# Gated layer with overlapping tiles and ternary matrices on three engines, statistics-operation norms, and first keys split over VectorE and ScalarE with joined stores

## The reference

```python
def _layernorm(x, axis=-1, eps=1e-05):
    m = jnp.mean(x, axis=axis, keepdims=True)
    v = jnp.var(x, axis=axis, keepdims=True)
    return (x - m) / jnp.sqrt(v + eps)
...
        q = _fq_sym(q, axis=-1)
        k = _fq_sym(k, axis=-1)
        v = _fq_sym(v, axis=2)
...
            w_dq = jnp.clip(jnp.round(w / gamma_w), -1.0, 1.0) * gamma_w
...
        gate = jax.nn.silu(bit_linear(x, gate_w, gate_b))
        val = bit_linear(x, val_w, val_b)
        return bit_linear(gate * val, out_w, out_b)
```

## Time and profile before

| | us |
|---|---|
| median of 3 runs | 6873.82 |
| lowest, highest | 6869.46, 6882.35 |
| profiled execution, its own time | 6872.02 |
| its span in the trace | 6870.2 |
| busy PE, DVE, ACT, POOL | 5802.4, 5704.3, 4387.7, 3741.3 |

### The profile page before, as it was taken

The page is one execution under the profiler, slowest core; times in us unless marked ns, Lnnn a source line. Parts: engine busy times, 40 slices in busy tenths (PEclk is TensorE's granted clock), DMA queues, the critical chain, the costliest instruction groups (busy, mean ns, idle before and its releaser), DMA issues. The chain is left out here.

```text
span 6870.2 us, 178673 instructions
## 1 busy us (share of the span) xinstructions
PE 5802.4 (84%) x63503; PEld 2380.6 (35%) x63510; DVE 5704.3 (83%) x8942; ACT 4387.7 (64%) x4251; POOL 3741.3 (54%) x3973
## 2 busy tenths in 40 slices
PE   2771699999999999999999999999949487999523
PEld 2331133333333333333333333333334353544311
DVE  5886699999999999999999999999943556777655
ACT  0330089988989889989889989989912013666301
POOL 2331078888888888878888888888810001000000
PEclk7995599999999999999999999999969697999756
DMA  1442211011011011011011011011020078877500
GB/s 57 112 108 94 46 22 18 9 26 19 9 26 19 9 26 18 10 26 18 10 26 18 11 25 19 11 25 19 10 48 0 19 303 181 116 112 114 85 28 9
DMA packets 182852, 319.86 MB, mean 47 GB/s; under 512 B 97220, under 2 KB 143813, under 8 KB 176803
## 3 DMA queue, kind: packets, MB, share of 16 engines
q1 hardware_dynamic: 181944, 307.93, 21.0%
HBM read 196.59 MB, written 113.33 MB: 45 GB/s over the span
## 5 line engine op out<-in xcount | busy, mean ns | idle before, releaser
L1024 DVE TENSOR_REDUCE a_mx<-PS 128x1 f32<-128x512 f32 x6620 | 4073.2, 688 | 230.1 <-PE PS L908 226.5
L995 ACT ACTIVATE a_e<-PS,a_sk 126x1024 f32<-126x1024 f32 x3264 | 3634.0, 1114 | 458.2 <-PE PS L893 109.6
L771 POOL TENSOR_SCALAR a_p<-a_e 126x1024 f16<-126x1024 f32 x3264 | 3418.1, 1047 | 641.0 <-ACT a_e L995 588.5
L908 PE MATMUL PS<-a_K,a_Q 48*128 48x512 bf16 (+1 forms) x6884 | 2109.8, 383 | 49.9 <-DMA a_K<-d_inv 49.9
L893 PE MATMUL PS<-a_Q,a_K 54*126 54x512 bf16 x6528 | 2113.3, 404 | 26.6 <-issue 17.4
L935 PE MATMUL PS<-a_e,a_sel 126*32 126x256 f32 x26112 | 1994.7, 382 | 0.0
L893 PEld LDWEIGHTS PS<-a_Q,a_K 54*126 54x126 bf16 x6528 | 615.4, 131 | 1377.3 <-issue 1319.6
L931 PE MATMUL PS<-a_p,a_V 128*32 128x256 f16 x13056 | 960.1, 284 | 14.1 <-ACT a_og L976 10.0
L931 PEld LDWEIGHTS PS<-a_p,a_V 128*32 128x32 f16 x13056 | 336.8, 93 | 1251.6 <-POOL a_p L771 1059.0
L935 PEld LDWEIGHTS PS<-a_e,a_sel 126*32 126x32 f32 x26112 | 756.1, 110 | 8.9 <-issue 2.4
L1891 DVE TENSOR_REDUCE b_mx<-PS 128x1 f32<-128x512 f32 x803 | 504.8, 685 | 188.4 <-PE PS L1775 188.4
(11 more groups left out here) (300 smaller groups left out, 3363.9 us busy)
## 6 DMA issues: line engine op xcount, KB each, us to landing
b_K<-d_k SPq DMA_DIRECT2D x210, 200.1 KB, 6.1
a_K<-d_k SPq DMA_DIRECT2D x102, 400.2 KB
d_v<-v1v SPq DMA_DIRECT2D x9, 3328.0 KB, 10.3
b_V<-d_v SPq DMA_DIRECT2D x36, 832.0 KB, 12.1
d_k<-k_T SPq DMA_DIRECT2D x400, 63.0 KB, 1.7
d_k<-k1p SPq DMA_DIRECT2D x54, 400.2 KB, 7.7
a_V<-d_v SPq DMA_DIRECT2D x68, 204.0 KB, 2.8
d_v<-vq SPq DMA_DIRECT2D x17, 803.2 KB
```

The source lines that it names most:

```text
L771: g.tensor_scalar(p[0:rows, kk % RE, :], e[0:rows, kk % RE, :], 1.0, SHIFT, ALU.mult, ALU.add).then_inc(rounded, 1)
L908: last = pe.matmul(self.PS[:, M_BANK + j % sh.SLOTS, c0:c0 + wd], Qb[M_ROWS, ii % 4, t * P:(t + 1) * P], Kb[M_ROWS, (ii // NC) % 2, k0:k0 ...
L995: a.activation(e[0:r, kk % RE, :], self.PS[0:r, e_bank(i, s):e_bank(i, s) + 2, :], ACT.Exp, scale=skb[0:r, hb, s:s + 1]).then_inc(exp_done, 1)
L1024: v.tensor_reduce(mx[:, col:col + 1], bank, AX.X, ALU.max).then_inc(max_done, 1)
```

## The change

Norms: 16 statistics operations and 16 aggregations give mean and variance, and 16 instructions apply both. First keys: the key scales are found straight from PSUM; a third, bf16 product of three bias rows adds the bias on TensorE; both bf16 casts and the copies of the values (plain and absolute) go to ScalarE; VectorE keeps a running largest value; the turn of a group comes one group later; the four parts share two banks, and a group is stored by three DMAs. First values: the largest values come from the running ones, are turned by TensorE and spread by a product with ones; scaling, rounding and storing go by halves and heads. First attention: the first keys come in five pieces, and GpSimd clears the 34 semaphores of the stages so far ahead of its buffers. Gated layer: the three matrices have buffers of their own, ScalarE scales them, GpSimd clips them, all beside the norm; in the main loop ScalarE takes the value half from PSUM, GpSimd adds its bias, and product and final step of a tile come one tile later.

```diff
+    def norm_sums(self, v, nm):
+        for t in range(self.sh.NT):
+            self.mark(v.bn_stats(nm["parts"][:, t, :], self.x[:, t, :]), self.dv)
+        v.wait_ge(self.dv, self.count[id(self.dv)])
+        for t in range(self.sh.NT):
+            self.mark(v.bn_aggr(nm["mean_var"][:, t, :], nm["parts"][:, t, :]), self.dv)
+        v.wait_ge(self.dv, self.count[id(self.dv)])
+        v.tensor_scalar(nm["st"][:, 2, :], nm["mean_var"][:, :, 1], EPS, None, ALU.add).then_inc(self.var_ready, 1)
...
+            self.mark(v.tensor_scalar(xn[:, t, :], self.x[:, t, :], nm["mean_var"][:, t, 0:1], st[:, 0, t:t + 1],
+                                      ALU.subtract, ALU.mult), self.dv)
...
+                    for c in range(2):
+                        sp.dma_start(self.d_k0[:, 8 * c:8 * c + 8, :, g * GW:g * GW + n].rearrange("i h d n -> (h d) i n"),
+                                     kT[:, g % 2, :, c, 0:n]).then_inc(stored[g % 2], 16)
...
+                    for y in range(2):
+                        for j, n in tiles(g):
+                            kv = self.PS[0:n, 2 * (g % 2) + y, j * D:(j + 1) * D]
+                            for c in range(2):
+                                pe.matmul(kv, cT[:, g % RC, c, j * KT:j * KT + n], W[:, c, y * D:(y + 1) * D],
+                                          start=(c == 0), stop=False)
+                            last = pe.matmul(kv, pick[0:96, 0:n], bp[0:96, y * D:(y + 1) * D], start=False, stop=True)
...
+                        self.link(v, v.tensor_reduce(sc, by_head(ps), AX.X, ALU.max, apply_absolute_value=True), self.dv)
...
+                    v.wait_ge(cast, 2 * g + 1)
+                    for s, n in spans(g):
+                        self.link(v, v.tensor_tensor(tmp2[0:n, b, s, :], kf[0:n, b, s, :], parts[0:n, b, HI, s, :], ALU.subtract), self.dv)
+                    v.sem_inc(to_cast, 1)
...
+                def largest(g):
+                    v.wait_ge(v_taken, g + 1)
+                    for s, n in spans(g):
+                        top = self.v_top[0:n, s, :]
+                        self.link(v, v.tensor_tensor(top, v_abs[0:n, g % 2, s, :], top, ALU.max), self.dv)
...
+                    scales(g)
+                    if g >= 1:
+                        rest(g - 1)
+                    whole(g)
+                    if g >= 1:
+                        last(g - 1)
+                    scaled(g)
+                    largest(g)
+                rest(NG - 1)
+                last(NG - 1)
...
+                    a.wait_ge(to_cast, 2 * g + 1)
+                    a.activation(parts[0:KT, g % 2, HI, :, :], kf[0:KT, g % 2, :, :], ACT.Copy).then_inc(cast, 1)
...
+                        ins = a.activation(parts[0:n, g % 2, MID, s, :], tmp2[0:n, g % 2, s, :], ACT.Copy)
...
+                        a.activation(self.v_raw[0:n, g * GT + s.start:g * GT + s.stop, :], ps, ACT.Copy)
+                        ins = a.activation(v_abs[0:n, g % 2, s, :], ps, ACT.Abs)
+                    ins.then_inc(v_taken, 1)
...
+                for g in range(NG):
+                    if g >= 3:
+                        evacuate(g - 3)
+                    if g >= 1:
+                        high(g - 1)
+                    values(g)
+                    if g >= 1:
+                        middle(g - 1)
...
-                L(v.tensor_reduce(mx[:, :], self.v_raw[:, :, :].rearrange("p t d -> p d t"), AX.X, ALU.max,
-                                  apply_absolute_value=True))
-                v.sem_inc(part_max, 1)
+                L(v.tensor_tensor(self.v_top[:, 0, :], self.v_top[:, 0, :], self.v_top[:, 1, :], ALU.max))
+                v.sem_inc(top_ready, 1)
                 L(v.memset(cs[:, :, :], 0.0))
-                L(v.tensor_copy(ident[:, :], self.idf[:, :]))
+                v.wait_ge(top_turned, 1)
+                L(v.tensor_reduce(top[:, :], self.PS[:, 2, 0:2 * P].rearrange("p (c k) -> p c k", c=2)[:, :, 0:KT], AX.X, ALU.max))
+                for c in range(2):
+                    L(v.tensor_scalar(spread[:, c, :], self.idf[:, :], top[:, c:c + 1], None, ALU.mult))
+                v.sem_inc(spread_ready, 1)
...
-                L(v.tensor_tensor(self.v_raw[:, :, :], self.v_raw[:, :, :], along(rv[:, :], 1, NKT), ALU.mult))
                 for c in range(2):
+                    w = slice(c * P, (c + 1) * P)
+                    L(v.tensor_tensor(self.v_raw[:, :, w], self.v_raw[:, :, w], along(rv[:, w], 1, NKT), ALU.mult))
                     v.wait_ge(zeroed, 2)
-                    if c == 1:
-                        v.wait_ge(stored, 16 * 9)
-                        v.wait_ge(summed, 1)
                     for h in range(8):
-
+                        if c == 1:
+                            v.wait_ge(stored, 16 * 9)
+                            v.wait_ge(summed, 1)
                         L(v.tensor_scalar(vq[:, h, :, 0:HD], self.v_raw[:, :, (8 * c + h) * HD:(8 * c + h + 1) * HD],
                                           ROUND, ROUND, ALU.add, ALU.subtract))
-                    v.sem_inc(half, 1)
+                        v.sem_inc(done, 1)
...
+                for s in self.early_sems:
+                    g.sem_clear(s)
...
+                for i in range(FIRST):
+                    k0, k1 = i * sh.WHOLE // FIRST * BANK, (i + 1) * sh.WHOLE // FIRST * BANK if i < FIRST - 1 else sh.NK
+                    for row, part in M_KEYS:
+                        sp.dma_start(Kb[row:row + HD, 0, k0:k1], self.d_k0[part, 0, :, k0:k1]).then_inc(ld_first[i], 16)
                 load_scales(sp, 0, 0)
-                for at in range(6):
+                for at in range(3, 6):
                     load_k(sp, 0, 0, at)
                 load_inv(sp, 0, 0)
                 load_q(sp, 0, 1, 1)
+                for i in range(FIRST):
+                    sp.wait_ge(ld_first[i], FIRST_LOADED[i])
+                sp.sem_inc(ld_k[0], 16 * 3)
...
+                    if first and j in range(0, sh.WHOLE, sh.WHOLE // FIRST):
+                        pe.wait_ge(ld_first[j // (sh.WHOLE // FIRST)], FIRST_LOADED[j // (sh.WHOLE // FIRST)])
...
-                        L(v.tensor_scalar(gw[:, i, 2:3], self.PS[:, 0, 0:1], 1.0 / (D * F), 1e-5, ALU.mult, ALU.max))
-                        L(v.reciprocal(gw[:, i, 3:4], gw[:, i, 2:3]))
-                        L(v.tensor_scalar(wf[:, :], wf[:, :], gw[:, i, 3:4], None, ALU.mult))
-                        L(v.tensor_scalar(wf[:, :], wf[:, :], ROUND, ROUND, ALU.add, ALU.subtract))
-                        L(v.tensor_scalar(tern[i][:, :], wf[:, :], -1.0, 1.0, ALU.max, ALU.min))
...
+                    self.norm_sums(v, nm)
+                    for i in range(3):
+                        v.wait_ge(ld[i], 16)
+                        L(v.tensor_reduce(gw[:, i, 0:1], wf[:, i, :], AX.X, ALU.add, apply_absolute_value=True))
+                        L(v.tensor_scalar(gw[:, i, 1:2], gw[:, i, 0:1], 1.0, None, ALU.mult))
+                        v.sem_inc(part, 1)
+                    for i in range(3):
+                        v.wait_ge(summed, i + 1)
+                        L(v.tensor_scalar(gw[:, i, 2:3], self.PS[:, i, 0:1], 1.0 / (D * F), 1e-5, ALU.mult, ALU.max))
+                        L(v.reciprocal(gw[:, i, 3:4], gw[:, i, 2:3]))
+                        v.sem_inc(scale_ready, 1)
+                    self.norm_apply(v, nm, xn)
...
+                        a.activation(wf[:, i, :], wf[:, i, :], ACT.Identity, bias=rnd[:, 0:1], scale=gw[:, i, 3:4]).then_inc(shifted, 1)
...
+                        g.tensor_scalar(wf[:, i, :], wf[:, i, :], ROUND, -1.0, ALU.subtract, ALU.max).then_inc(clipped, 1)
+                        g.wait_ge(clipped, 2 * i + 1)
+                        g.tensor_scalar(tern[i][:, :], wf[:, i, :], 1.0, None, ALU.min).then_inc(clipped, 1)
...
-                        rest(t)
+                        turn(t)
+                        if t >= 1:
+                            back(t - 1)
+                    back(NT - 1)
...
+                    def front(t):
+                        a.wait_ge(gv_ps, t + 1)
+                        if t >= 2:
+                            a.wait_ge(h_ready, t - 1)
+                        a.activation(vt[:, t % 2, :], self.PS[:, 2:4, :].rearrange("p b n -> p (b n)"), ACT.Copy,
+                                     scale=st[:, 2, t:t + 1]).then_inc(v_taken, 1)
                         a.wait_ge(g_ready, t + 1)
                         a.activation(gt[:, t % 2, :], gt[:, t % 2, :], ACT.Silu).then_inc(g_act, 1)
+                    front(0)
+                    for t in range(NT):
+                        if t + 1 < NT:
+                            front(t + 1)
...
+                        g.wait_ge(v_taken, t + 1)
+                        g.tensor_tensor(vt[:, t % 2, :], vt[:, t % 2, :], vb[:, :], ALU.add).then_inc(v_ready, 1)
...
-                        L(v.scalar_tensor_tensor(out=vt[:, t % 2, :], in0=flat(2), scalar=st[:, 2, t:t + 1], in1=vb[:, :],
```

(6 more changed lines are left out.)

361 lines of the change are left out of this document (213 added, 148 removed).

## The result

The changed kernel takes 6716.4 us (median of four runs, 6713.4 to 6719.3) against 6871.6 us (6865.4 to 6882.4) before: ratio 0.9772, 95% interval 0.9756 to 0.9789. That is 2.3% faster, where 3.5% was forecast. 6716 lies 80 us above the forecast of 6636. It is 54 above the top of the forecast's own range (6662) and 31 above the top of the range that also covers the main rivals (6685). The profiled execution's span is 6711.5 us, 158.7 less than before.

What follows compares the result with a forecast made beforehand. TensorE, 98% busy, fills the untouched first attention loop (4184 of 6870 us); changed short stages follow one another. Gains 47 + 68 + 18 + 26.6 + 39 + 39 = 237.6 off 6872.0, plus 1.8, give 6636 us, range 6610 to 6662.

Steps and rivals of the forecast that it cites:

- the main rivals: TensorE taking over in the first keys (chance 0.17) and full clock in the gated loop (0.14); range 6590 to 6685.
- First values: Stage after the first keys: one chain of waits, shortened from 150 to 82 us, gain 68 us.
- Gated layer ahead of its loop: Work before the gated loop: norm, scaling and clipping beside VectorE's quantizing; gain 39 us, 33 to 42.
- Gated loop: Loop of the gated layer: evacuation wait and L2099 leave the chain, 2.55 us a tile; gain 39 us.
- The rival of a full clock in this loop: Gated loop: TensorE at full clock, two more us saved in each of 16 tiles; 6604, down to 6590; chance 0.14.
- Attention loop: Loop of the first attention, 4184 us: body unedited, so no change; moving over 10 us would make the prediction wrong.
- first keys: First stage, VectorE-bound: group period from 7.46 to 6.3 us over fifty periods, less new costs; gain 47 us.
- its rival: First keys: TensorE takes over, period 7.0 instead of 6.3, +35 us; 6671, up to 6690; chance 0.17.
- the slower one: First keys: TensorE drops to 1.2 GHz and stays; at period 11.5 the kernel takes about 6890; chance 0.01.
- The start of the attention: First attention: TensorE starts at about 12 us instead of 29.8, after GpSimd's clears; gain 18 us, 14 to 21.
- The norms: Norms: 12.9 us each instead of 22.4; together 26.6 us gained, the expert layer's norm giving 7.6.
- The rival "not what it says": GpSimd's clearing and VectorE's scaling collide throughout, or norm statistics cost their upper bounds: 8 + 15 less gain, 6659; chance 0.04.

## Why the prediction was wrong, step by step

**First values: the step was "combining maxima, the turn, the spreading product and the limits are eight small instructions, about 4.7 us".** It was short by 18 us, because two of them, the spreads, got no turn until GpSimd had cleared. I had asked whether the clearing slows the large scaling and priced that at 8 us. The scaling was untouched, and a 0.29 us operation ahead of it bore the whole. With the spreading in another form the stage takes 83 us; 82 were forecast. The rest of this chain was right.

**Gated layer ahead of its loop: the step was GpSimd's clipping "under the cover of VectorE's quantizing. Uncovered by 20% slowing it would cost nothing, by 60% some 4 us".** It made a slowing of GpSimd the only risk. In fact VectorE, which sets the end, was held: 16 applications took 40.9 us and not 4.3. The 2.1 us a pass from the earlier trace rows did not hold beside VectorE either; the passes took 5.4 and 7.1. With the clips on VectorE the stage is 28 us shorter: that accounts for the shortfall, with the 7.4 us that the clips then cost.

**Gated loop: the step was "GpSimd's bias add has a whole tile's time".** It has, and the estimate of 2.2 us for it was good (2.34). But I looked at when it ends, not at what it shuts out while it runs. It starts 0.4 us ahead of the product and adds 1.79 us to it. Without this meeting the loop gains 44.7 us; the forecast of 39 was a little low. What left the chain did leave: no wait for the evacuation, and a turn of 1.03 us. The rival of a full clock in this loop had no ground: the granted clock went from 0.60 to 0.63. One reading of the prediction was off without harm to the sum: VectorE's 127 us are 53% of the 241, so it was busy just over half of the loop.

**Attention loop: "The diff leaves its body alone, so I leave this time alone too."** The body kept its work and lost its place in the program. None of the rivals had this, and the prediction named 10 us of movement as what would refute it: 28.9.

**Where it was right.** The group starts of the first keys lie 6.26 us apart, with the short wait for ScalarE that was forecast (0.25 us where 0.3 was; timeline, two groups):

```profile
155.90 0.69 DVE L559 TENSOR_REDUCE k_scales<-PS 126x32 f32<-126x512 f32 x1
...
159.72 0.74 DVE L593 TENSOR_TENSOR k_parts<-k_tmp,k_parts 126x512 bf16<-126x512 f32 x1 [0.25 <-ACT k_parts L625]
162.16 0.69 DVE L559 TENSOR_REDUCE k_scales<-PS 126x32 f32<-126x512 f32 x1
```

Over all groups the mean is 6.24 instead of 7.46, which makes 60.6 us. The new work ahead of the first group costs 5.1 (6.5 forecast). The tail, forecast 3.5 us longer, is 2.0 shorter, perhaps because the casts left VectorE there as well; that wasn't tried. Together this puts the stage 10.7 us above its forecast. TensorE did not take over; from the first to the last group it ran at a granted clock of 1.00 where it had 0.91, so neither its rival nor the slower one had ground.

The start of the attention went as forecast, and GpSimd's clearing released TensorE:

```profile
595.59 2.00 PE L1061 MATMUL PS<-a_K,a_Q 48*128 48x512 bf16 x4 [29.88 <-POOL a_p L880]
```

That is 10.3 us into the stage (12 forecast, 29.8 before). The remaining 7 us of this term were luck. They came from a wait of GpSimd with the label "issue" ahead of its first small step, at 860.86 in the kernel before, which is gone after. It may be a wait for its program, but it wasn't tried and stays open.

The norms take 12.6 us (12.9 forecast) and divide otherwise than I had it: statistics 0.33 us from start to start (5.3 for sixteen), aggregations 0.07 (1.2), applications 5.3 instead of 4.0. The 6.8 us that the prediction worked out as a second value for the statistics was too high by 1.5.

**The sum.** The four missed terms make -98 us, keys, attention start and norms +18 or 19; together some -80, the distance between forecast and result. Of the +18, 7 us are the unexplained wait of GpSimd and 5.5 the shorter tail, which no step of the prediction had; without this luck the miss would have been over 90 us. The rival "not what it says" had the right pair of engines, but bounded their collision at 8 us in one stage. It was some 70 in three (16.8 + 27.9 + 24.0 by the runs). A range is only as good as the bound of its least known term, and this one had been taken from a slowing in proportion, which no row showed.

## What to carry to other kernels

When work moves to GpSimd, list for each of its instructions what VectorE does in the same microseconds. A `tensor_scalar` of VectorE over many columns, from SBUF to SBUF, waited for the end of whatever GpSimd instruction was running (a clearing, a clip or an addition). An operation with two inputs in SBUF waited for an addition, which reads, and not for a clearing, which only writes. So give GpSimd short instructions, or gate them with a semaphore so that they fall beside VectorE's reductions, its reads of PSUM or its idle time. And a loop that is not edited can still move: look at the waits called "issue" at its jump back, before and after.

## What the runs showed of the hardware

- Where VectorE and GpSimd get in each other's way, they exclude each other for whole instructions, whichever starts first. A 0.29 us operation waited 18.8 us for a clearing of 21.86, and took 2.7 to 2.8 us when the clearing came in pieces of 2.8; GpSimd waited for VectorE as well (3.15 us instead of 2.35). Not held beside GpSimd: VectorE's two-input operations beside a clearing, its maxima (1.22 us), its reciprocal (1.75), a `tensor_scalar` on one column (0.15), its `tensor_scalar` that reads PSUM (0.42 for 256 columns, as without GpSimd), and ScalarE.
- TensorE stops at a loop's jump back: 2.9 us per turn in the best place seen, 3.9 and 4.4 us in the worst. With 64 instructions more ahead of the loop the second stop was gone, with 256 more it was there, and 217 more brought it into the kernel before. The page after lists 559 packets with 9.16 MB on its larger instruction queue, some 16.4 KB each, which fits the 16384 bytes of the expectations. If such a packet holds the 256 instructions after which the place repeats, an instruction has 64 bytes (an estimate). That the stop is the wait for such a packet fits all four places, but the packets themselves were not changed alone.
- A semaphore clear on GpSimd took some 65 ns (34 in the 2.2 us between the stage's start and the first of its small clearings), where 0.1 us had been assumed.
